# Attention block kernel, one core: the last batch's norms and the epilogue rewritten

## The chip, the cores and the metric

One core of one Trainium2 chip runs the kernel. The metric is device microseconds of one execution; before the change three runs gave 4011.88, 4012.55 and 4014.0 us (median 4012.55).

## The reference

For each of 16 images x (512 channels, 1024 pixels), all in float32:

```
qkv  = w_qkv @ x                       # 1536 x 512, then q, k, v: 8 heads of 64
sim  = (q * 64**-0.5)^T k              # per head, 1024 x 1024
out  = softmax(sim) v
y    = w_out @ out + b_out             # 512 x 1024
y    = y * rsqrt(mean_c(y*y) + 64**-0.5) * rms_scale[c]
return y + x
```

## The kernel before

One batch is one image. A batch is cut into 8 slots: a slot is a pair of heads and one half (512) of the 1024 query pixels (slot = 2 * pair + half). A slot has 16 places t = 0..15, and every engine has its own program, written out by hand, that walks the same slots and places and meets the others through semaphores. Nothing is planned at run time; what an engine does is in the order in which its function `one(body)` issues it.

In a slot TensorE (PE) makes the scores of key tile j at place t = 2j (`scores`, lines 642 and 651: 4 matmuls for 2 heads), and the products of probabilities and values at t = 1, 5, 9 and 13 (`values`, L664, two key tiles each). The last two key tiles of a slot are multiplied at t = 1 of the next slot, followed by `sums` (L583): two matmuls of ones with `prob_sum`, which give each head's softmax denominators. ScalarE (ACT) makes the exponentials (L734), two of 128x512 per key tile. GpSimd (POOL) adds the probabilities up (L1093, L1097): 14 additions of 128x512 per slot, the last ones for key tile 7. VectorE (DVE) finds row maxima of the next slot's scores, inverts the sums (L994, two reciprocals of 128x256), and makes `o_norm` (L1001). `o_norm` is split into two fp32r parts, `o_hi` by ACT (L803) and `o_lo` (L329) by POOL, in slot 6 by DVE.

The output projection of a slot is done in the slot after it, at t = 11: items O0 and O1 (L558), six fp32r matmuls each; DVE adds their result to `y_sb` (L970, 128x1024 each). So y of half 0 of a batch is complete in slot 7, y of half 1 in slot 0 of the next batch. Then come the norm's steps: four squares by ACT (L818) into `sq_a`, `sq_b`, `o_norm` and `inv_sum`; three additions by POOL (`add_squares`, L1105); a matmul of a constant 1/512 with the sum; `+ SCALE` by DVE (L981); two reciprocals (L988); a square root by ACT (`root`, L837, which loads the table of Sqrt and afterwards, L839, that of Exp); y times scale times root (L1007 on DVE, or prescaled by ACT and multiplied by POOL); residual added by POOL into `resid` (L1128), which SyncE (SP) had loaded from x (L399) and stores from there (L405). In the bodies of the 16 batches all of this lies beside the next batch's attention.

After the last batch's slot 7 nothing lies beside it: that is the epilogue, the code behind `run_bodies` in each engine's function (items R0, O0, O1, R1). In it PE does the last values, R0 (the mean of squares of half 0, one fp32 matmul on `sq_a`, L572), `sums`, O0 and O1, R1. DVE does R0's addend and reciprocals, then the sums' reciprocals from the copy that ACT made (`copy_sums`, L797), `o_norm`, four scalings of half 0, two y additions, then R1 and four scalings of half 1. POOL adds the squares of half 0, splits `o_lo`, adds the residuals of half 0, adds the squares of half 1 and adds its residuals. SP loads and stores half 0, then half 1 in the same `resid` tile.

The places before in the last batch's slot 7: `o_hi` at t = 6, `o_lo` on POOL ahead of key tile 4's additions, O0 and O1 at t = 11, squares at t = 13 and 14.

Of the kernel before, what the change touches and what calls it, by code (L numbers as in the profile page):

```python
# [13 lines left out]
P = 128  # L14
# [48 lines left out]

def items_at(slot, t, first, last):
# [22 lines left out]
    if t == 11:  # L87
        if preceding:
            out += [("O0", 0), ("O1", 2)]
# [38 lines left out]
def attention_kernel(nc, x, wqkv, wout, bias, scale, consts, out):  # L128
# [27 lines left out]
    with ctx:  # L156
# [94 lines left out]
        resid_added = sem("resid_added")  # L251
        resid_loaded = [sem(f"resid_loaded{i}") for i in range(MT)]
# [73 lines left out]
        def split_output_low(eng, done):  # L326
# [3 lines left out]
                              ).then_inc(olo_ready, 1)  # L330

# [24 lines left out]
        def _(sp):  # L356
# [100 lines left out]
        def _(pe):  # L457
# [44 lines left out]
            def item(body, slot, name, turn=None):  # L502
# [58 lines left out]
                else:  # L561
# [107 lines left out]
            def one(body):  # L669
                for slot in range(SLOTS):  # L670
# [3 lines left out]
                    for t in range(PLACES):  # L674
# [4 lines left out]
                        elif t % 4 == 1:  # L679
                            for j in (2 * g - 2, 2 * g - 1):  # L680
# [35 lines left out]
            item(last, 0, "R0")  # L716
# [7 lines left out]
        def _(act):  # L724
# [121 lines left out]
            def one(body):  # L846
                for slot in range(SLOTS):
                    for t in range(PLACES):
# [17 lines left out]
                        if t == OUTPUT_HIGH_AT[slot] and not (body.first and slot == 0):  # L866
                            split_output_high(body.b * SLOTS + slot, body)
# [3 lines left out]
                        for half in range(2):  # L871
                            if (slot, t) in SQUARE_AT[half] and (half == 0 or not body.first):
                                for m in range(MT):
                                    if (slot, t) == SQUARE_AT[half][m]:
                                        square(body, half, m)
# [22 lines left out]
            copy_sums(B * SLOTS, 0)  # L898
            root(2 * (B - 1))
# [3 lines left out]
            root(2 * (B - 1) + 1)  # L903
# [3 lines left out]
        def _(dve):  # L907
            def item(body, slot, name):
# [62 lines left out]
                elif name[0] == "R":  # L971
# [4 lines left out]
                    if name == "R1":  # L976
                        dve.wait_ge(y_scaled, scaled_before(batch, 0, 0, False) + MT)
# [41 lines left out]
            def one(body):  # L1019
                for slot in range(SLOTS):  # L1020
                    preceding = not (body.first and slot == 0)
                    for t in range(PLACES):
# [13 lines left out]
                        if t == OUTPUT_HIGH_AT[slot] and slot not in LOW_BY_GPSIMD:  # L1036
# [181 lines left out]
```

## Time and profile before

| | us |
|---|---|
| median of three runs | 4012.55 |
| the profiled execution's own time | 4015.77 |
| its span, first to last instruction | 4013.7 |
| PE busy / DVE / ACT / POOL | 3947.8 / 2890.3 / 2319.8 / 2920.6 |
| last values matmul of the last batch ends | 3969.2 |
| last probability addition on POOL ends | 3970.1 |
| last instruction on POOL (a residual addition) ends | 4011.2 |

Rows of a timeline give start, duration, engine, line, operation, output<-input, shape and count; the brackets hold how long the engine was idle before and who released it. Neighbouring instructions of one kind are merged, so that an "x4" row's duration is that of all four. PEclk is the granted TensorE clock, 1.00 for 2.4 GHz and 0.50 for 1.2 GHz.

### The profile page before, as it was taken

To read this page: it belongs to the slowest core of one execution; us is meant where nothing else is said; L and a number is where in the kernel's file an instruction comes from. 1 tells how busy PE (TensorE), PEld (TensorE's weight loads), DVE (VectorE), ACT (ScalarE), POOL (GpSimd) and SP (SyncE) were. 2 spreads that over 40 slices of the span, in tenths; PEclk is the share of its full clock that TensorE was granted. 3 is DMA by queue.
4 is the path that set the end of the run, shared out by engine and by line. 5 is a ranking of instruction groups with operands and counts; after the bars stand their busy time and mean duration, and the time that the engine had idled before them with its cause. 6 is when DMAs were issued, how large, how long until landed. Compare 5 with 4: busy or idle time off the path is not lost.

```text
span 4013.7 us, 53763 instructions
## 1 busy us (share of the span) xinstructions
PE 3947.8 (98%) x18624; PEld 2423.5 (60%) x18624; DVE 2890.3 (72%) x3279; ACT 2319.8 (58%) x4044; POOL 2920.6 (73%) x2279
## 2 busy tenths in 40 slices
PE   8999999999999999999999999999999999999996
PEld 5566665666666666666666666666566666666652
DVE  6677777777767777677777776777777777677765
ACT  4556565565655656565565655656556565565653
POOL 5678677686876768677686776867678677786866
PEclk9999999999999999999999999999999999999997
DMA  4111111111111201102011111111111111111100
GB/s 149 47 48 53 43 66 50 43 57 39 69 48 43 74 30 66 53 35 71 32 63 53 37 69 46 50 53 49 59 51 53 43 64 53 43 53 43 69 17 32
DMA packets 71275, 212.22 MB, mean 53 GB/s; under 512 B 8152, under 2 KB 8280, under 8 KB 58208
## 3 DMA queue, kind: packets, MB, share of 16 engines
q1 hardware_dynamic: 71008, 208.80, 14.8%
q8 instruction: 151, 2.47, 0.3%
q14 instruction: 116, 0.95, 0.1%
HBM read 168.92 MB, written 39.85 MB: 52 GB/s over the span
## 4 chain that ended last, share of the span: by engine, by line
PE 94%; DVE 3%; issue 2%; POOL 1%; ACT 0%; DMA 0%; SPq 0%; POOLq 0%; ACTq 0%; DVEq 0%
PE pv L664 23%; PE aux L498 17%; PE score L642 14%; PE score L651 11%; PE aux L532 9%; PE aux L558 9%; PE aux L627 6%; PE pv L583 3%; PE aux L608 2%; DVE inv_sum L994 1%; DVE maxima L936 1%; DVE k_l L929 1%; DVE y_sb L1007 0%; DVE aux L942 0%; ACT probs L734 0%
## 5 line engine op out<-in xcount | busy, mean ns | idle before, releaser
L1097 POOL TENSOR_TENSOR prob_sum<-prob_sum,probs 128x512 f32<-128x512 f32 x1536 | 1967.2, 1308 | 375.6 <-ACT probs L734 374.2
L734 ACT ACTIVATE probs<-score 128x512 f32<-128x512 f32 x2048 | 1109.1, 594 | 864.0 <-PE score L651 856.5
L942 DVE TENSOR_REDUCE aux<-aux 128x1 f32<-128x513 f32 x640 | 446.9, 698 | 836.4 <-PE aux L627 636.3
L664 PE MATMUL pv<-probs,v_sb 128*64 128x512 f32 x4096 | 993.5, 606 | 0.0
L642 PE MATMUL score<-q_hl,k_hh 128*128 128x512 f32 x2048 | 868.1, 424 | 5.8 <-ACT probs L734 5.8
L651 PE MATMUL score<-q_hm,k_l 72*128 72x512 f32 x2048 | 815.0, 398 | 0.2 <-DVE q_hm L954 0.2
L1093 POOL TENSOR_TENSOR prob_sum<-probs 128x512 f32<-128x512 f32 x256 | 338.3, 1342 | 492.4 <-ACT probs L734 492.4
L498 PE MATMUL aux<-x_hi,w_ring 128*128 128x512 f32 x2048 | 658.0, 398 | 9.7 <-DMA scale_sb<-scale 8.9
L642 PEld LDWEIGHTS score<-q_hl,k_hh 128*128 128x128 f32 x2048 | 386.9, 189 | 267.3 <-issue 154.3
L664 PEld LDWEIGHTS pv<-probs,v_sb 128*64 128x64 f32 x4096 | 248.4, 136 | 483.0 <-issue 435.3
L936 DVE TENSOR_REDUCE maxima<-aux 128x1 fp32r<-128x1024 f32 x384 | 466.3, 1214 | 0.0
L948 DVE TENSOR_REDUCE maxima<-aux 128x1 fp32r<-128x512 f32 x640 | 442.3, 691 | 22.0
L994 DVE RECIPROCAL inv_sum<-inv_sum 128x256 f32<-128x256 f32 x256 | 440.9, 1738 | 10.0 <-ACT inv_sum L797 6.5
L498 PEld LDWEIGHTS aux<-x_hi,w_ring 128*128 128x128 f32 x2048 | 386.5, 189 | 93.5 <-DMA scale_sb<-scale 8.9
L651 PEld LDWEIGHTS score<-q_hm,k_l 72*128 72x128 f32 x2048 | 388.9, 190 | 60.5 <-DVE q_hm L954 0.7
L498 PE MATMUL aux<-x_lo,w_ring 128*128 128x512 f32 x1024 | 401.1, 392 | 0.0
L532 PE MATMUL aux<-w_ring,x_hi 128*128 128x256 f32 x1984 | 361.2, 282 | 0.0
L532 PEld LDWEIGHTS aux<-w_ring,x_hi 128*128 128x128 f32 x1984 | 316.2, 191 | 11.6
L627 PEld LDWEIGHTS aux<-k_hh,q_hm 64*128 64x128 f32 x762 | 112.1, 184 | 320.2 <-issue 244.2
L627 PE MATMUL aux<-k_hh,q_hm 64*128 64x512 f32 x762 | 278.0, 444 | 10.0 <-DVE k_l L929 10.0
L532 PE MATMUL aux<-w_ring,x_lo 128*128 128x256 f32 x992 | 280.2, 283 | 0.0
L627 PE MATMUL aux<-k_hh,q_hl 64*128 64x512 f32 x762 | 277.6, 444 | 0.0
(94 smaller groups left out, 5013.1 us busy)
## 6 DMA issues: line engine op xcount, KB each, us to landing
w_ring<-w_split SPq DMA_DIRECT2D x93, 1024.0 KB, 4.8
x_stage<-x SPq DMA_DIRECT2D x128, 256.0 KB, 4.3
resid<-x SPq DMA_DIRECT2D x128, 256.0 KB, 4.2
out<-resid SPq DMA_DIRECT2D x128, 256.0 KB, 2.0
w_split<-w_ring SPq DMA_DIRECT2D x3, 1024.0 KB, 12.6
w_split<-y_sb SPq DMA_DIRECT2D x3, 1024.0 KB, 3.9
y_sb<-wqkv SPq DMA_DIRECT2D x4, 512.0 KB, 9.0
probs<-wqkv SPq DMA_DIRECT2D x2, 512.0 KB, 8.9
```

The costliest lines, as they stand in the source:

```text
L498: last = pe.matmul(out_ap, w[:, wp, k, cols], xp[:, k, xcols], start=(k == 0 and n == 0), stop=(k == KT - 1 and n == 2))
L532: last = pe.matmul(to[:, i * WCOLS:(i + 1) * WCOLS], xp[:, c, jt * P:(jt + 1) * P], w[:, wp, c, :], start=(n == 0), stop=(n == 3 * KT - 1))
L627: last = pe.matmul(bank(k + h), q_hi_at(nhalf, e, h, it), k_hh[rows, npair % 2, e, h * HALF:(h + 1) * HALF], start=True, stop=True)
L642: pe.matmul(score[e][:], k_hh[:, pair % 2, e, keys], q_hl[:, half, e, :], start=True, stop=False)
L651: pe.matmul(score[e][:], k_l1[0:D + 2 * IT, pair % 2, e, keys], q_hm[0:D + 2 * IT, half, e, :], start=False, stop=True).then_inc(score_rea ...
L664: pe.matmul(pv[half][e * D:(e + 1) * D, :], v_sb[:, pair // 2, j, (pair % 2) * P + e * D:(pair % 2) * P + (e + 1) * D], probs[:, j % 4, e, ...
L734: act.activation(probs[:, j % 4, e, :], score[e][:], ACT.Exp, scale=SOFT).then_inc(prob_ready, 1)
L936: dve.tensor_reduce(maxima[:, n:n + 1], bank(k, 2), AX_X, ALU.max).then_inc(aux_free[k], 1)
L942: dve.tensor_reduce(aux[:, first:first + 1], aux[:, k * HALF:first + 1], AX_X, ALU.max).then_inc(aux_free[k], 1)
L948: dve.tensor_reduce(maxima[:, n:n + 1], bank(k), AX_X, ALU.max).then_inc(aux_free[k], 1)
L994: dve.reciprocal(inv_sum[:, cols], inv_sum[:, cols]).then_inc(inv_ready, 1)
L1097: pool.tensor_tensor(prob_sum[:, e, :], prob_sum[:, e, :], probs[:, j % 4, e, :], ALU.add).then_inc(prob_added, 1)
```

## The change

Two constants move work within the last batch's slot 7, and the epilogue is written anew. In the last slot `o_hi` is made at t = 5, `o_lo` by DVE instead of POOL, O0 and O1 run at t = 9 ahead of the values, all four squares of half 0 at t = 9 in ACT's order, and R0 at t = 13. DVE adds the squares of half 0 (`add_squares` became a shared helper). In the epilogue ACT loads the Sqrt table once, prescales both halves of y (four operations each), and takes the last root in two column halves; DVE inverts the sums straight from PSUM, splits `o_lo`, and for half 1 does the multiplication by the root and the residual addition itself, in two column halves of 128x(4x256); the residual rows for it come into `x_stage`, a buffer of their own. R1 is four matmuls that accumulate the four squares. POOL does the multiplications and residual additions of half 0 alone.

```diff
+LAST_HIGH_AT = 5
+LAST_OUTPUT_AT = 9
@@ items_at
-    if t == 11:
+    if t == (LAST_OUTPUT_AT if last and slot == SLOTS - 1 else 11):
@@ helpers
+        def output_high_at(body, slot):
+            return LAST_HIGH_AT if body.last and slot == SLOTS - 1 else OUTPUT_HIGH_AT[slot]
+        def low_by_gpsimd(body, slot):
+            return slot in LOW_BY_GPSIMD and not (body.last and slot == SLOTS - 1)
+        def add_squares(eng, done):
+            for m in range(1, MT):
+                eng.wait_ge(sq_made, 4 * done + m + 1)
+                if m > 1:
+                    eng.wait_ge(sq_added, 3 * done + m - 1)
+                eng.tensor_tensor(sq_a[:], sq_a[:], squares[m][:], ALU.add).then_inc(sq_added, 1)
@@ sync
-            for half in range(2):
-                load_resid(B - 1, half)
-                store_half(B - 1, half)
-            wait_stored(2 * B)
+            load_resid(B - 1, 0)
+            for m in range(MT):
+                wait_piece(sp, KT + m, B - 1)
+                sp.dma_start(x_stage[:, m, :], x_v[B - 1, m, :, HALF:N]).then_inc(last_rows_loaded, 16)
+            store_half(B - 1, 0)
+            for part in range(2):
+                cols = slice(part * HALF // 2, (part + 1) * HALF // 2)
+                sp.wait_ge(last_rows_added, part + 1)
+                for m in range(MT):
+                    sp.dma_start(out_v[B - 1, m, :, HALF + part * HALF // 2:HALF + (part + 1) * HALF // 2],
+                                 x_stage[:, m, cols]).then_inc(out_stored[m], 16)
+            wait_stored(2 * B + 1)
@@ tensor, item R0 / R1
-                        pe.wait_ge(sq_added, 3 * (2 * batch + half + 1))
-                        pe.matmul(bank(k), ones_c[:].bitcast(F32), sq_a[:], start=True, stop=True
-                                  ).then_inc(aux_full[k], 1)
+                        if name == "R0":
+                            pe.wait_ge(sq_added, 3 * (2 * batch + half + 1))
+                        parts = squares[:1] if name == "R0" else squares
+                        for m, part in enumerate(parts):
+                            if name == "R1":
+                                pe.wait_ge(sq_made, 4 * (2 * batch + half) + m + 1)
+                            last = pe.matmul(bank(k), ones_c[:].bitcast(F32), part[:],
+                                             start=(m == 0), stop=(m == len(parts) - 1))
+                        last.then_inc(aux_full[k], 1)
@@ tensor, one(body), t % 4 == 1
+                            if "O0" in names:
+                                item(body, slot, "O0")
+                                item(body, slot, "O1")
                             for j in (2 * g - 2, 2 * g - 1):
...
+                            if body.last and slot == SLOTS - 1 and g == BLOCKS - 1:
+                                item(Body(epi, B - 1, False, True), 0, "R0")
@@ tensor, epilogue
-            item(last, 0, "R0")
             sums(end, 0)
@@ scalar, one(body)
-                            if (slot, t) in SQUARE_AT[half] and (half == 0 or not body.first):
...
+                                at = SQUARE_AT[half][m]
+                                if body.last and half == 0:
+                                    at = (SLOTS - 1, LAST_OUTPUT_AT)
+                                if (slot, t) == at and (half == 0 or not body.first):
+                                    square(body, half, m)
@@ scalar, epilogue
-            copy_sums(B * SLOTS, 0)
-            root(2 * (B - 1))
+            act.activation(table_back[:], ones_d[:, 0:1], ACT.Sqrt)
+            act.wait_ge(inv_ms_ready, 2 * (2 * (B - 1) + 1))
+            act.activation(rms_a[:], rms_b[:], ACT.Sqrt).then_inc(rinv_ready, 1)
+            for m in range(MT):
+                act.wait_ge(sq_made, 4 * 2 * (B - 1) + m + 1)
+                act.activation(y_sb[:, 0, m, :], y_sb[:, 0, m, :], ACT.Identity, scale=scale_sb[:, m:m + 1]
+                               ).then_inc(y_prescaled, 1)
             split_output_high(B * SLOTS)
             for m in range(MT):
                 square(end, 1, m)
-            root(2 * (B - 1) + 1)
...
+            for part in range(2):
+                cols = slice(part * HALF // 2, (part + 1) * HALF // 2)
+                act.wait_ge(inv_ms_ready, 2 * (2 * (B - 1) + 1) + part + 1)
+                act.activation(rms_a[:, cols], rms_b[:, cols], ACT.Sqrt).then_inc(rinv_ready, 1)
@@ vector, item R1
-                        dve.wait_ge(y_scaled, scaled_before(batch, 0, 0, False) + MT)
+                        dve.wait_ge(y_scaled_by_pool, scaled_before(batch, 0, 0, True) + MT)
@@ vector, epilogue
+            add_squares(dve, 2 * (B - 1))
             item(last, 0, "R0")
             for part in range(2):
                 invert(last, 0, "R0", part)
+            dve.wait_ge(sums_ready, B * SLOTS)
             for part in range(2):
-                invert_sums(end, 0, part)
+                cols = slice(part * HALF // 2, (part + 1) * HALF // 2)
+                dve.reciprocal(inv_sum[:, cols], pv[0][:, cols]).then_inc(inv_ready, 1)
             normalise(end, 0)
-            for m in range(MT):
-                scale_y(end, 0, m)
+            split_output_low(dve, B * SLOTS)
             for name in ("O0", "O1"):
                 item(end, 0, name)
             item(last, 0, "R1")
             for part in range(2):
                 invert(last, 0, "R1", part)
-            for m in range(MT):
-                scale_y(end, 1, m)
+            dve.wait_ge(y_prescaled, scaled_before(B - 1, 0, 0, True) + 2 * MT)
+            for part in range(2):
+                cols = slice(part * HALF // 2, (part + 1) * HALF // 2)
+                y = y_sb[:, 1, :, cols]
+                dve.wait_ge(rinv_ready, 2 * (B - 1) + 1 + part + 1)
+                dve.tensor_tensor(y, y, rms_a[:, cols].unsqueeze(1).to_broadcast([P, MT, HALF // 2]), ALU.mult
+                                  ).then_inc(y_scaled, 1)
+                dve.wait_ge(y_scaled, scaled_before(B - 1, 0, 0, False) + part + 1)
+                dve.wait_ge(last_rows_loaded, 16 * MT)
+                dve.tensor_tensor(x_stage[:, :, cols], x_stage[:, :, cols], y, ALU.add).then_inc(last_rows_added, 1)
@@ gpsimd, epilogue
-            add_squares(2 * (B - 1))
-            split_output_low(pool, B * SLOTS)
...
+            pool.wait_ge(rinv_ready, 2 * (B - 1) + 1)
+            scaled = scaled_before(B - 1, 0, 0, True)
+            for m in range(MT):
+                pool.wait_ge(y_prescaled, scaled + m + 1)
+                pool.tensor_tensor(y_sb[:, 0, m, :], y_sb[:, 0, m, :], rms_a[:], ALU.mult
+                                   ).then_inc(y_scaled_by_pool, 1)
+                pool.wait_ge(y_scaled_by_pool, scaled + m + 1)
+                pool.wait_ge(resid_loaded[m], 16 * (2 * (B - 1) + 1))
+                pool.tensor_tensor(resid[:, m, :], resid[:, m, :], y_sb[:, 0, m, :], ALU.add
+                                   ).then_inc(resid_added, 1)
```

## Rows read from the trace of the kernel before

**Rows 1.** The page: the chain that ended last, shares by engine.

```profile
PE 94%; DVE 3%; issue 2%; POOL 1%; ACT 0%; DMA 0%; SPq 0%; POOLq 0%; ACTq 0%; DVEq 0%
```

**Rows 2.** Windows: stretch, length, busy us (instructions) by engine, clock, DMA share, GB/s.

```profile
3855.00:3900.00 45.00, 44.77 (x198) 25.38 (x194) 31.67 (x37) 24.51 (x43) 26.48 (x22) 1.00 0.00 1
3942.00:3953.00 11.00, 9.96 (x27) 4.05 (x29) 3.90 (x5) 3.61 (x7) 3.40 (x4) 0.69 0.00 0
3953.00:3985.00 32.00, 19.69 (x70) 8.22 (x66) 12.55 (x11) 12.49 (x22) 20.88 (x17) 0.82 0.00 0
3985.00:4013.70 28.70, 6.45 (x14) 3.74 (x14) 15.66 (x13) 6.10 (x9) 17.57 (x12) 0.56 0.31 110
```

**Rows 3.** Timeline of PE, slot 7 of the last batch and the epilogue.

```profile
3945.39 3.68 PE L664 MATMUL pv<-probs,v_sb 128*64 128x512 f32 x8
...
3960.39 0.47 PE L558 MATMUL aux<-o_hi,wo_hi 128*128 128x512 f32 x1 [0.23 <-POOL o_lo L329]
...
3967.24 1.94 PE L664 MATMUL pv<-probs,v_sb 128*64 128x512 f32 x8
3974.62 2.05 PE L572 MATMUL aux<-sq_a,ones_c 128*128 128x512 f32 x2 [5.44 <-POOL sq_a L1105]
3976.59 1.98 PE L583 MATMUL pv<-prob_sum,ones_d 128*64 128x512 f32 x4
3987.33 0.77 PE L558 MATMUL aux<-o_hi,wo_hi 128*128 128x512 f32 x1 [8.76 <-POOL o_lo L329]
...
3990.41 0.40 PE L558 MATMUL aux<-o_hi,wo_lo 128*128 128x512 f32 x1
...
3997.22 2.04 PE L572 MATMUL aux<-sq_a,ones_c 128*128 128x512 f32 x2 [5.49 <-POOL sq_a L1105]
```

**Rows 4.** Timeline of DVE, the same stretch.

```profile
3954.23 0.69 DVE L1001 TENSOR_TENSOR o_norm<-inv_sum,pv 128x512 f32<-128x512 f32 x1
3962.06 2.58 DVE L970 TENSOR_TENSOR y_sb<-y_sb,aux 128x1024 f32<-128x1024 f32 x2 [7.14 <-PE aux L558]
...
3980.71 3.31 DVE L994 RECIPROCAL inv_sum<-inv_sum 128x256 f32<-128x256 f32 x2
3984.05 0.69 DVE L1001 TENSOR_TENSOR o_norm<-inv_sum,pv 128x512 f32<-128x512 f32 x1
...
3991.77 1.22 DVE L970 TENSOR_TENSOR y_sb<-y_sb,aux 128x1024 f32<-128x1024 f32 x1 [0.28 <-PE aux L558]
...
4000.03 3.37 DVE L988 RECIPROCAL rms_b<-rms_a 128x256 f32<-128x256 f32 x2
```

**Rows 5.** Timeline of ACT, the same stretch.

```profile
3979.29 1.28 ACT L837 ACT_TABLE_LOAD   x1
...
3984.77 0.63 ACT L803 ACTIVATE o_hi<-o_norm 128x512 fp32r<-128x512 f32 x1 [1.80 <-DVE o_norm L1001]
3991.52 0.63 ACT L818 ACTIVATE sq_a<-y_sb 128x512 f32<-128x512 f32 x1 [6.12 <-DVE y_sb L970]
...
4003.42 0.63 ACT L837 ACTIVATE rms_a<-rms_b 128x512 f32<-128x512 f32 x1 [7.95 <-DVE rms_b L988]
```

**Rows 6.** Timeline of POOL, the same stretch.

```profile
3960.18 9.96 POOL L1097 TENSOR_TENSOR prob_sum<-prob_sum,probs 128x512 f32<-128x512 f32 x8
...
3985.48 1.71 POOL L329 TENSOR_TENSOR o_lo<-o_norm,o_hi 128x512 fp32r<-128x512 f32 x1 [11.01 <-ACT o_hi L803]
```

**Rows 7.** Durations of DVE operations with two SBUF inputs: ns min/median/max, first and last start.

```profile
L1016 DVE TENSOR_TENSOR w_ring<-y_sb,w_ring x2: 1226/1226/1226, 6.3 to 11.5; 128x1024 fp32r<-128x1024 f32 x2
L1007 DVE SCALAR_TENSOR_TENSOR y_sb<-y_sb,scale_sb,rms_a x8: 744/1248/1759, 3984.7 to 4007.1; 128x512 f32<-128x512 f32 x8
L329 DVE TENSOR_TENSOR o_lo<-o_norm,o_hi x16: 1681/1773/1775, 234.1 to 3931.2; 128x512 fp32r<-128x512 f32 x16
```

**Rows 8.** Timeline of SP's queue: four loads, and the last store.

```profile
3993.44 1.99 SPq L399 DMA_DIRECT2D resid<-x  x4
...
4011.20 0.33 SPq L405 DMA_DIRECT2D out<-resid  x1
```

More of the change, by code:

```diff
@@ L865, in one @@
                             repeat_queries(body, slot)
-                        if t == OUTPUT_HIGH_AT[slot] and not (body.first and slot == 0):
+                        if t == output_high_at(body, slot) and not (body.first and slot == 0):
                             split_output_high(body.b * SLOTS + slot, body)
@@ L902, in _ @@
                 square(end, 1, m)
-            root(2 * (B - 1) + 1)
+            for m in range(MT):
+                act.wait_ge(sq_made, 4 * (2 * (B - 1) + 1) + m + 1)
+                act.activation(y_sb[:, 1, m, :], y_sb[:, 1, m, :], ACT.Identity, scale=scale_sb[:, m:m + 1]
+                               ).then_inc(y_prescaled, 1)
+            for part in range(2):
+                cols = slice(part * HALF // 2, (part + 1) * HALF // 2)
+                act.wait_ge(inv_ms_ready, 2 * (2 * (B - 1) + 1) + part + 1)
+                act.activation(rms_a[:, cols], rms_b[:, cols], ACT.Sqrt).then_inc(rinv_ready, 1)
         @block.vector
@@ L1035, in one @@
                                     scale_y(body, half, m)
-                        if t == OUTPUT_HIGH_AT[slot] and slot not in LOW_BY_GPSIMD:
+                        if t == output_high_at(body, slot) and not low_by_gpsimd(body, slot):
                             split_output_low(dve, body.b * SLOTS + slot)
@@ L1098, in add_probs @@
                                            ALU.add).then_inc(prob_added, 1)
-            def add_squares(done):
-                for m in range(1, MT):
-                    pool.wait_ge(sq_made, 4 * done + m + 1)
-                    if m > 1:
-                        pool.wait_ge(sq_added, 3 * done + m - 1)
-                    pool.tensor_tensor(sq_a[:], sq_a[:], squares[m][:], ALU.add).then_inc(sq_added, 1)
             def split_squares_low(done):
@@ L1120, in add_resid @@
                 done = 2 * batch + half
-                if body.plan is epi:
-                    pool.wait_ge(y_scaled, scaled_before(batch, 0, 0, False) + MT * half + m + 1)
-                elif m in SCALE_BY_GPSIMD[half]:
+                if m in SCALE_BY_GPSIMD[half]:
                     pool.wait_ge(y_scaled_by_pool, scaled_before(batch, half, m, True) + 1)
@@ L1133, in one @@
                     for j in range(STEPS):
-                        if j == OUTPUT_LOW_AT and slot in LOW_BY_GPSIMD and not (body.first and slot == 0):
+                        if j == OUTPUT_LOW_AT and low_by_gpsimd(body, slot) and not (body.first and slot == 0):
                             split_output_low(pool, body.b * SLOTS + slot)
@@ L1138, in one @@
                         elif slot in ADD_SQUARES_IN and not body.first:
-                            add_squares(2 * (body.b - 1) + slot)
+                            add_squares(pool, 2 * (body.b - 1) + slot)
                         if not body.last:
@@ L1169, in _ @@
             run_bodies(pool, one)
-            add_squares(2 * (B - 1))
-            split_output_low(pool, B * SLOTS)
-            end = Body(epi, B, False, True)
+            pool.wait_ge(rinv_ready, 2 * (B - 1) + 1)
+            scaled = scaled_before(B - 1, 0, 0, True)
             for m in range(MT):
-                add_resid(end, 0, m)
-            add_squares(2 * (B - 1) + 1)
-            for m in range(MT):
-                add_resid(end, 1, m)
+                pool.wait_ge(y_prescaled, scaled + m + 1)
[5 more added lines that the diff above has]
+                                   ).then_inc(resid_added, 1)
 def kernel(x, L0_conv_w_qkv, L0_conv_w_out, L0_conv_b_out, L0_conv_rms_scale):
```

5 lines of the change are left out of this document (2 added, 3 removed).

## The prediction

> **What bounds the kernel now.** I read the page's chain of waits first: 94% of it is PE [rows 1]. In a body window PE is busy 44.77 of 45 us (the first of [rows 2]), so bodies 0 to 14 are PE's, and the edit issues the same instructions there. I give them zero. What is left is the last batch's slot 7 and what follows. The windows say who is short there: from 3953 to 3985 PE is busy 19.69 of 32 us, from 3985 to the end 6.45 of 28.7, and no engine is busy throughout [rows 2]. This stretch is a chain of single steps, so every step on it counts in full. From the timelines I read the chain (times in the span, each start + duration):
>
> 1. POOL finishes the probability sums at 3960.18 + 9.96 = 3970.14 [rows 6].
> 2. PE could now do `sums`, but R0 stands ahead of it in PE's queue and waits for POOL's three additions of squares: 3974.62. `sums` ends at 3978.57 [rows 3].
> 3. DVE has R0's reciprocals ahead of the sums' reciprocals, which start at 3980.71; `o_norm` ends at 3984.74 [rows 4], `o_hi` at 3985.40 [rows 5], POOL's `o_lo` at 3987.19 [rows 6].
> 4. PE: O0 and O1 from 3987.33; R1 from 3997.22, behind three more POOL additions, until 3999.26 [rows 3].
> 5. DVE's reciprocals end at 4003.40 [rows 4], the root at 4004.05 [rows 5]; then four scalings and four residual additions overlap, and the last store is issued at 4011.20 [rows 8], 2.5 us before the span's end at 4013.7.
>
> **The change, part by part.**
>
> *Slot 7 (o_hi at t=5, o_lo on DVE, O0/O1 at t=9, squares behind them, R0 at t=13).* `o_norm` is there at 3954.92 [rows 4]; `o_hi` takes 0.63; `o_lo` on DVE beside a busy POOL takes 1.77 [rows 7]: 3957.35. O0 starts then instead of at 3960.39 [rows 3] and moves ahead of values 2 and 3. DVE's y additions began 1.67 us after O0's start and took 2.58 [rows 3, 4]: they end at 3961.6. Two squares are done by then, two more take 0.6 each: ACT is free at 3962.8, and it is now that key tile 5's scores are ready (values 2, 3 of 1.94 us behind O1's end at 3960.2, then 0.8 us for two score matmuls of about 0.4). So the squares cost ACT almost nothing, but key tile 6's scores wait for ACT: about 0.5 us. R0 is one fp32 matmul in two passes: 2.05 us at the low clock [rows 3], where values of 3.68 us at the low clock take 1.94 at the high one, so 1.05 here. It stands ahead of key tile 7's scores. All in all the last exponentials end at about 3969.5, and POOL's two last additions (9.96 / 8 = 1.25 each) at 3971.6, which is 1.5 later than now. Ends of the range: 3968.9 (POOL has lost an `o_lo` of about 1.3, and nothing else changes) and 3973.1 (four DVE operations each hold up POOL by some 0.5 us, and R0 waits besides). I take 3971.6. DVE's additions of squares cost 0.75 to 1.76 each (least and most of L1007 in [rows 7]); from 3961.7 they end between 3964.5 and 3967, R0 is due at 3966.6: hidden, just. R0's addend (0.69) and reciprocals (3.37) [rows 4] then lie between 3967.7 and 3971.8, beside the POOL additions.
>
> *Sums to O0.* `sums` follows the probabilities directly. PE is idle about 1 us before it, after which I expect the high clock: 1.05 us, against 1.98 at the low one [rows 3]: 3972.75. The reciprocals read PSUM directly; ACT's copy, which took 0.6, is gone. No row shows a reciprocal from PSUM. DVE's y additions with a PSUM operand take the 1.22 us that two SBUF operands take [rows 4, 7], so I take 3.31 for both, with 3.0 and 4.0 as ends. DVE starts them at 3972.8 instead of 3980.71: **7.9 us gained**. `o_norm` 0.69 and `o_hi` 0.63 are as before (ACT has long finished its root and prescalings, 3971.8 + 0.63 + 4 x 0.63 = 3975). `o_lo` is DVE's instead of POOL's: beside POOL's multiplications 1.77, alone 0.75, against 1.71 now [rows 6, 7]. I take 1.77, since POOL has eight operations of 1.25 to 1.71 to do from 3973 on, so O0 starts 7.9 earlier too: S = 3979.4.
>
> *O0 to R1.* Now: O0 at 3987.33, R1's end at 3999.26, so S + 11.9. After: the first square ends at 3992.15 [rows 5], S + 4.8, and R1's first matmul starts. Values of 1.94 us are two fp32 full-array equivalents, 0.92 each, and 1.75 each at the low clock [rows 3]. Four in a row are 3.7 or 7.2 us: S + 8.5 or S + 12.0. The three POOL additions ahead of R1 go. The clock decides: before, PE restarted at 3987.33 and ran at 0.40 us matmuls from 3990.41, 3.1 us later [rows 3]. Now the pause before R1 is under 1 us instead of 5.5, so I expect most of R1 at the high clock and allow half a microsecond: S + 9.0. **2.9 gained**; ends 3.4 and -0.1.
>
> *R1 to the end.* DVE's addend and reciprocals are as before (4.14 us from R1's end). Its wait for `y_scaled_by_pool` holds nothing up: POOL's fourth multiplication comes at about 3985, R1's addend at 3988. Now the rest is 4013.7 - 4003.40 = 10.3 us. After: the first half of the root lies beside the second reciprocal, the second beside the first multiplication. DVE does four operations of 128x1024 with two SBUF operands and POOL idle, 1.23 each [rows 7], 5.1 with gaps. The last four stores wait for the last of them together; DMA issues on SP are 0.33 [rows 8] and up to 1.99 / 4 = 0.5 apart, so the fourth is issued 1.35 us behind the first. The tail behind the last store is now 2.5; half the bytes save up to 0.3 or, as rows of 1 KB instead of 2 KB, nothing. 5.1 + 1.35 + 2.35 = 8.8. **1.5 gained**; ends 2.3 and 0. Part 0's stores go out 2.5 us earlier and are off the queue. The new x_stage loads (4 issues, 2 us of SP) and half 0's stores (its last residual addition about 3986) end long before. The Exp table load at the end is beside DVE's work in both.
>
> The Trainium skill (SBUF — State Buffer, "SBUF: two separate sides") says that a DVE operation with two SBUF inputs and a GpSimd operation that reads SBUF exclude each other for the whole instruction. The trace agrees: DVE's L1007 takes 744 ns at the least and 1759 at the most, `o_lo` on DVE beside POOL 1773 [rows 7]. It speaks against giving `o_lo` and the squares' additions to DVE; what that is worth is the third rival below.
>
> **The sum.** 7.9 + 2.9 + 1.5 = 12.3. The profiled execution's own time is 4015.77 for a span of 4013.7; I leave the 2.1 us outside the span as they are, and 4001.4 of span is 4003.5 of own time. The median of the runs is 3.2 lower than the profiled one, so the forecast is 4012.55 - 12.3 = **4000.3 us**.
>
> **Rivals.**
> - *R1 and sums at the low clock.* For it: the clock was 0.56 over the last 28.7 us, and just ahead of slot 7's second key tile it was 0.69 over 11 us although PE was busy for 9.96 of them [rows 2]. Against: the pause before R1 nearly goes. Price 3.0 (R1) + 0.9 (sums) = 3.9: 4004.2.
> - *The edit doesn't do what "one table load" says.* Squares, copies and scalings under the Sqrt table are in no row; if they need tables of their own, each change is a load of 1.28 us [rows 5]. Against it: now no load stands ahead of the squares after an Exp. Two on the chain: 4002.9.
> - *Port and queue in slot 7.* Each of the four DVE operations added there takes up to 1.77 and holds POOL, whose ten microseconds of additions set the slot's end [rows 6]; R0, if late, holds PE and key tile 7's scores. Decides when the squares' additions end behind 3966.6. Price 1.5 to 4: about 4003.
> - *Slower: the clock falls in slot 7 and stays down.* Place: PE waits for `o_lo` at t=9 and for ACT at key tile 6. If these pauses drop the clock at about 3957, as happened ahead of 3945.39 (values 3.68 instead of 1.94 [rows 3]), twelve microseconds of PE work take up to 22, and with sums and R1 low as well (3.9) the loss is 14: 4014, against before 1.5 slower. It needs the low clock through the whole slot; the clock seen there was back at 3953 [rows 2], and an episode of 7 us costs 3.5 and the kernel still faster. For it speaks little: the pauses here are 0.5 us, and O0's wait of 0.23 in the slot left the clock up [rows 3].
>
> **How the numbers follow.** What a measurement of this kernel can tell from no change is 0.2%, 8 us. Forecast 0.64; low clock in the tail 0.14; table loads 0.04; port and queue 0.09; slot at the low clock 0.03; 0.06 for disturbances of the bodies that no row shows (both signs). Best ends together (`o_lo` 1.0, R1 0.5, slot 0.7, tail 0.8): 3997.3; a range that leaves out 2 in 10 goes up to the low clock with a tail that gives nothing, 4005.5. The forecast's own range is 3998 to 4002.5. Faster by over 8 us means under 4004.5: forecast, table and most of the others, 0.85. Within: half of the low clock case, part of the port's and of the slot case: 0.11. Slower by over 8 us: 0.04.
>
> **What would show it.** O0 of slot 7 at about 3957.4; R0 done before 3968 with no wait on DVE's additions; last probability addition 3971.6; `sums` about 1 us; its reciprocals at 3972.8; O0 at 3979.4; PEclk at 1.00 in R1 and its end at 3988.4; last store issued about 3999; span 4001.4. Wrong would be it if R0 waits, if R1 takes 7 us, if the reciprocals from PSUM take over 4, or if the four halves' operations are well over 1.25 each.

## The result, and the profile after

The changed kernel takes 4000.53 us (median of 7 runs, 3997.39 to 4005.26), the kernel before 4014.0 in the same 7 rounds (4011.58 to 4014.86). The ratio is 0.997, 95% interval 0.996 to 0.9981. The gain is 13.5 us by the medians, where 12.3 were forecast. The span of the profiled execution went from 4013.7 to 3998.3.

These 15.4 us of span are not all the edit's. Some two and a half of them had come by the time slot 7 of the last batch was under way. That is drift from run to run: in the twelve traces with the same instructions up to there, the mark named here lies between 3947.85 and 3952.65. From 50 to 3930 us the granted clock was 1.00 in every window of 500 us or less, in all fourteen traces; in three of them it was 0.97 over the first 50 us, and the stretch just ahead of the mark took 12.56 to 15.31 us in the twelve (see "And the turn" below), so two parts of the drift are episodes of the clock. So I measure from one mark, the start of the values of key tiles 0 and 1 in that slot, to the end of the span, and call it the tail. The mark in the kernel before and in the changed one (PE timeline, columns as in the rows ahead of the prediction; the first block is the kernel before, the second the changed one):

```profile
3952.65 1.94 PE L664 MATMUL pv<-probs,v_sb 128*64 128x512 f32 x8
```

```profile
3950.19 1.94 PE L700 MATMUL pv<-probs,v_sb 128*64 128x512 f32 x8
...
3954.74 0.47 PE L587 MATMUL aux<-o_hi,wo_hi 128*128 128x512 f32 x1
...
3963.97 1.13 PE L607 MATMUL aux<-sq_a,ones_c 128*128 128x512 f32 x2
...
3968.97 1.08 PE L619 MATMUL pv<-prob_sum,ones_d 128*64 128x512 f32 x4 [1.08 <-POOL prob_sum L1162]
3976.51 0.76 PE L587 MATMUL aux<-o_hi,wo_hi 128*128 128x512 f32 x1 [6.46 <-DVE o_lo L336]
...
3981.50 1.07 PE L607 MATMUL aux<-sq_a,ones_c 128*128 128x512 f32 x2
...
3984.61 1.02 PE L607 MATMUL aux<-inv_sum,ones_c 128*128 128x512 f32 x2
```

The tail is 4013.7 - 3952.65 = 61.05 us before and 3998.3 - 3950.19 = 48.11 after: 12.94 less. In PE's rows the reader sees where: R0 (L607) now lies inside the slot without a wait, `sums` follows the last probability addition and takes 1.08 us instead of 1.98 [rows 3], and R1's four matmuls begin as soon as O1 ends instead of after 5.49 us. DVE's rows of the changed kernel, which answer to [rows 4]:

```profile
3953.14 1.46 DVE L336 TENSOR_TENSOR o_lo<-o_norm,o_hi 128x512 fp32r<-128x512 f32 x1 [0.70 <-ACT o_hi L843]
...
3958.92 1.12 DVE L350 TENSOR_TENSOR sq_a<-sq_a,sq_b 128x512 f32<-128x512 f32 x1
...
3960.94 0.69 DVE L350 TENSOR_TENSOR sq_a<-sq_a,inv_sum 128x512 f32<-128x512 f32 x1
...
3970.10 3.37 DVE L1127 RECIPROCAL inv_sum<-pv 128x256 f32<-128x256 f32 x2 [0.87 <-PE pv L619]
...
3974.89 1.48 DVE L336 TENSOR_TENSOR o_lo<-o_norm,o_hi 128x512 fp32r<-128x512 f32 x1 [0.70 <-ACT o_hi L843]
...
3986.39 3.37 DVE L1043 RECIPROCAL rms_b<-rms_a 128x256 f32<-128x256 f32 x2
...
3993.26 1.23 DVE L1144 TENSOR_TENSOR x_stage<-x_stage,y_sb 128x1024 f32<-128x1024 f32 x1
```

POOL, ACT and SP of the changed kernel, answering to [rows 5, 6, 8]:

```profile
3951.52 7.97 POOL L1162 TENSOR_TENSOR prob_sum<-prob_sum,probs 128x512 f32<-128x512 f32 x6
3960.98 7.94 POOL L1162 TENSOR_TENSOR prob_sum<-prob_sum,probs 128x512 f32<-128x512 f32 x6 [1.49 <-ACT probs L774]
```

```profile
3960.31 1.09 ACT L774 ACTIVATE probs<-score 128x512 f32<-128x512 f32 x2
...
3966.70 1.28 ACT L941 ACT_TABLE_LOAD   x1
```

```profile
3992.12 4.19 SPq L480 DMA_DIRECT2D out<-x_stage  x8
```

The one table load is the only one in the epilogue. The windows, answering to [rows 2], show PE and POOL busier in the same 32 us (23.63 and 24.90 us against 19.69 and 20.88), and POOL with nothing to do in the last 13 us:

```profile
3953.00:3985.00 32.00, 23.63 (x79) 12.01 (x78) 18.35 (x15) 16.12 (x29) 24.90 (x19) 0.84 0.09 33
...
3985.00:3998.30 13.30, 0.63 (x2) 0.00 (x0) 8.72 (x7) 2.39 (x5) 0.00 (x0) 0.61 0.24 79
```

### The profile page after: what moved, and what is told of

Same layout as the page of the kernel before. It is cut to its first block, busy times and chain, and to the rows that moved or that the text cites. A ratio compares the mean times of both kernels' runs of the same rounds, so it can differ in the third digit from the quotient of the medians.

```text
span 3998.3 us, 53773 instructions
## 1 busy us (share of the span) xinstructions
PE 3947.6 (99%) x18630; PEld 2424.4 (61%) x18630; DVE 2890.7 (72%) x3280; ACT 2319.5 (58%) x4048; POOL 2906.4 (73%) x2271
## 4 chain that ended last, share of the span: by engine, by line
PE 95%; DVE 3%; issue 1%; ACT 0%; DMA 0%; POOL 0%; SPq 0%; ACTq 0%; DVEq 0%; POOLq 0%
PE pv L700 23%; PE aux L527 17%; PE score L678 14%; PE score L687 11%; PE aux L561 9%; PE aux L587 9%; PE aux L663 6%; PE pv L619 3%; PE aux L644 2%; DVE inv_sum L1049 1%; DVE maxima L991 1%; DVE k_l L984 1%; DVE y_sb L1062 0%; DVE aux L997 0%; ACT probs L774 0%
## 6 DMA issues: line engine op xcount, KB each, us to landing
w_split<-w_ring SPq DMA_DIRECT2D x3, 1024.0 KB, 12.2
```

## The experiments

All are edits of the changed kernel. In the table times are in us and count from the mark; S is the start of O0 in the epilogue. Each row is one trace. From trace to trace the same code can differ by the clock: R1's end, for example, lies at S + 8.63 to S + 9.12 in the eight traces whose code from S to R1's end is the changed kernel's.

| kernel | reciprocals of sums | S | R1's end | R1's end to the end | tail |
|---|---|---|---|---|---|
| before | 28.06 | 34.68 | S + 11.93 | 14.44 | 61.05 |
| changed | 19.91 | 26.32 | S + 9.12 | 12.67 | 48.11 |
| changed, again | 19.93 | 26.34 | S + 8.98 | 12.65 | 47.97 |
| R1 on POOL's sum | 19.94 | 26.32 | S + 11.69 | 12.62 | 50.63 |
| slot 7 as before | 24.48 | 30.51 | S + 8.64 | 12.67 | 51.82 |
| and POOL adds half 0 | 28.04 | 34.07 | S + 8.63 | 12.70 | 55.40 |
| one part | 19.91 | 26.32 | S + 8.63 | 14.10 | 49.05 |
| R0 behind the slot | 21.93 | 27.97 | S + 8.63 | 12.69 | 49.29 |
| copied sums | 20.58 | 26.35 | S + 8.67 | 12.62 | 47.64 |
| copied, POOL paused | 20.60 | 26.37 | S + 9.09 | 12.63 | 48.09 |
| 24 more matmuls | 19.93 | 26.45 | S + 7.36 | 12.69 | 46.50 |
| combined | 19.92 | 25.55 | S + 7.36 | 12.33 | 45.24 |
| and the turn | 19.91 | 25.55 | S + 7.35 | 12.29 | 45.19 |
| and finer y | 19.92 | 25.55 | S + 6.42 | 12.30 | 44.27 |

**R1 on POOL's sum.**

```diff
-                        if name == "R0":
-                            pe.wait_ge(sq_added, 3 * (2 * batch + half + 1))
-                        parts = squares[:1] if name == "R0" else squares
+                        pe.wait_ge(sq_added, 3 * (2 * batch + half + 1))
+                        parts = squares[:1]
@@ gpsimd, epilogue, behind half 0
+            add_squares(pool, 2 * (B - 1) + 1)
```

> The changed kernel with R1 undone: POOL adds the squares of half 1, R1 is one matmul on sq_a. Measure: the tail, from the start of values 0 and 1 in the last slot 7 to the end of the span; it is 61.05 us before (4013.7 - 3952.65) and 48.1 after (3998.3 - 3950.19). Theory (each step of the chain counts in full): R1's end was O0's start + 9.1 in the changed kernel and + 11.9 before; the three additions come back, but the clock is still high for R1: + 10.9 to + 11.9, so tail 49.9 to 50.9. Rival (the three additions were beside something, or POOL is slow after its half 0 work): tail within 0.5 of 48.1, or over 52.

Tail 50.63, inside the theory's 49.9 to 50.9; median 4005.57 of 10 runs. One clause of the theory failed: the clock was not still high for R1. It waited for POOL and, after that pause, ran at the low clock:

```profile
3985.54 2.04 PE L604 MATMUL aux<-sq_a,ones_c 128*128 128x512 f32 x2 [5.00 <-POOL sq_a L350]
```

So squares summed by PE are worth 2.5 us, of which about one is the clock (2.04 for R1's single matmul, against 1.02 to 1.13 for each of the four).

**Slot 7 as before.**

```diff
-LAST_HIGH_AT = 5
-LAST_OUTPUT_AT = 9
+LAST_HIGH_AT = 6
+LAST_OUTPUT_AT = 11
...
+            item(last, 0, "R0")
             sums(end, 0)
```

> The changed kernel with slot 7 as before: o_hi at t=6, o_lo by POOL, O0 and O1 at t=11, squares at t=13 and 14, R0 behind the slot and ahead of sums; DVE still adds the squares and the epilogue is the new one. Theory: squares end 9.0 us behind those of the changed kernel (3969.0 against 3960.2, with 2.5 us of shift), R0 waits for DVE's third addition until about 18.5 us after the start of values 0 and 1, DVE's R0 reciprocals then stand ahead of the sums' ones, which start about 23.6 after it against 19.9 in the changed kernel: tail 51.8 (+3.7, up to +4.7 if R0 and sums run at the low clock). Rival (the whole 7.9 us came from the moves in slot 7): tail 56. Other rival (it came from DVE's additions and PSUM reads alone): tail within 1 of 48.1.

Tail 51.82, median 4005.24 of 10 runs. Both rivals are out (56, and within 1 of 48.1). That the theory's 51.8 is met to the tenth is luck: the reciprocals of the sums started at 24.48 and not at about 23.6, `sums` ran at the low clock (1.98 us), and what brought the tail back is that `o_lo` took 1.16 instead of 1.48 and that R1 ended at S + 8.64 instead of 9.12. DVE's additions beside a busy POOL took up to 2.21 us, R0 waited for them:

```profile
3961.75 2.21 DVE L350 TENSOR_TENSOR sq_a<-sq_a,sq_b 128x512 f32<-128x512 f32 x1 [1.39 <-ACT sq_b L854]
3964.24 1.40 DVE L350 TENSOR_TENSOR sq_a<-sq_a,o_norm 128x512 f32<-128x512 f32 x1 [0.28 <-ACT o_norm L854]
```

```profile
3967.46 1.36 PE L607 MATMUL aux<-sq_a,ones_c 128*128 128x512 f32 x2 [2.56 <-DVE sq_a L350]
```

**Slot 7 as before, and half 0's squares added by POOL.** The edit above, and `add_squares(pool, 2 * (B - 1))` in POOL's epilogue in place of DVE's.

> Slot 7 as before (like the second experiment) and half 0's squares added by POOL as before; sums still inverted straight from PSUM, the rest of the epilogue the changed one. Theory: POOL can add the squares only behind its last probability addition, R0 starts 22.0 us after values 0 and 1 (20.36 less 1.3 = 19.1 with DVE's additions), the sums' reciprocals at 28.1 instead of 24.5, tail 51.8 + 3.6 = 55.4. Rival (DVE's additions beside POOL, at 1.4 to 2.2 us each, are worth little): tail under 53.5.

Tail 55.40 and reciprocals at 28.04: both as expected, and the latter within 0.02 of the kernel before. One execution, 4007.44 us.

```profile
3972.25 2.04 PE L607 MATMUL aux<-sq_a,ones_c 128*128 128x512 f32 x2 [5.44 <-POOL sq_a L350]
```

PE's wait of 5.44 is the same as in [rows 3]. With this the 12.94 us are taken apart: 61.05 to 55.40 is the new epilogue (5.65), to 51.82 DVE's additions instead of POOL's (3.58), to 48.11 the moves in slot 7 (3.71). The last term is too small by the clock in R1: by S, which lies ahead of R1, the three are 0.61, 3.56 and 4.19, and the rest of the new epilogue's 5.65 lies behind S (3.30 up to R1's end, 1.74 after it). DVE's additions hold POOL up, too: POOL's last eight probability additions took 10.84 us in "slot 7 as before", with DVE's three beside them, and 9.96 here without.

**One part.** One root, one multiplication and one addition of 128x2048, four stores of 256 KB behind them, instead of two column halves.

```diff
-            for part in range(2):
+            for part in range(1):
-                cols = slice(part * HALF // 2, (part + 1) * HALF // 2)
+                cols = slice(0, HALF)
```

> The changed kernel with the last rows in one part: one root of 512 columns, one multiplication and one addition of 128x2048, four stores of 256 KB issued together at the end. Theory: the root (0.63) comes onto the chain in place of nothing, DVE's work stays at 4.8, and the last store is issued as before 1.2 to 1.5 behind the addition but moves twice the bytes, with all four behind each other on the queue (1 MB at 385 GB/s is 2.7 us, of which 1.3 us are behind the last issue): tail 48.1 + 0.6 + 1.2 = 49.9. Rival (column halves gain nothing since SP's issues set the end): tail 48.7 at most.

Tail 49.05, below the 49.9 of the theory and above the 48.7 of the rival. The tail mixes in R1, which in this execution met a better clock. From R1's end to the end it is 14.10 against 12.67: 1.43. DVE waited 0.76 for the root, and the stores end 0.78 later; DVE's own work is 0.2 shorter.

```profile
3987.70 2.29 DVE L1135 TENSOR_TENSOR y_sb<-y_sb,rms_a 128x2048 f32<-128x2048 f32 x1 [0.76 <-ACT rms_a L953]
```

**R0 behind the slot, alone.**

```diff
-                            if body.last and slot == SLOTS - 1 and g == BLOCKS - 1:
-                                item(Body(epi, B - 1, False, True), 0, "R0")
...
+            item(last, 0, "R0")
             sums(end, 0)
```

> The changed kernel with R0 alone moved behind the slot's last values (ahead of sums), everything else as changed. Theory: key tile 7's scores come 1.0 us earlier and so do the last exponentials and POOL's last addition, by 0.4 to 1.0; R0 lies in PE's pause before sums; but DVE's R0 addend and reciprocals (4.1 us) start about 1.9 us later, and the sums' reciprocals queue behind them: they start 21.6 to 22.0 us after the start of values 0 and 1 instead of 19.9, so tail 49.8 to 50.2. Rival (R0 in the slot only costs, since it holds key tile 7's scores): tail 47.1 to 47.7.

Tail 49.29 from one execution, half a microsecond below the 49.8 to 50.2 expected: the reciprocals start at 21.93 as expected, the rest is a little better (`o_lo` 1.17, R1's end at S + 8.63). But one part of my theory fell: the last additions of POOL did not come earlier. They start 10.78 us after the mark, as in the changed kernel (10.79), and run without a gap:

```profile
3960.69 7.92 POOL L1161 TENSOR_TENSOR prob_sum<-prob_sum,probs 128x512 f32<-128x512 f32 x6 [1.51 <-ACT probs L773]
```

R0 in the slot costs nothing, since from key tile 5 on POOL is behind. `sums` waits for POOL in both (0.87 here, 1.08 there).

**Copied sums.**

```diff
+            copy_sums(B * SLOTS, 0)
             act.wait_ge(inv_ms_ready, 2 * (2 * (B - 1) + 1))
@@ vector
-                dve.reciprocal(inv_sum[:, cols], pv[0][:, cols]).then_inc(inv_ready, 1)
+                invert_sums(end, 0, part)
```

> The changed kernel with the sums copied by ACT again before DVE inverts them (inv_sum <- pv, then reciprocals from SBUF). Theory: the copy stands on the chain, 0.6 us plus a hand-over, and a reciprocal costs the same from either memory (3.37 for both): tail 48.7. But R0's reciprocals end 0.9 before the sums do, so nothing else hides it. Rival (reading PSUM lengthened something else): tail 48.1 or less.

The tail was 47.64 in the one execution, where 48.7 was expected: a miss. The reciprocals began 0.67 later as expected and took 3.37 from either memory, yet S moved by 0.03 only, since `o_lo` was shorter (the rest of the 0.47 is R1, at S + 8.67 instead of 9.12). DVE, then POOL, of this kernel:

```profile
3968.84 3.37 DVE L1050 RECIPROCAL inv_sum<-inv_sum 128x256 f32<-128x256 f32 x2 [1.58 <-ACT inv_sum L837]
...
3973.62 0.83 DVE L336 TENSOR_TENSOR o_lo<-o_norm,o_hi 128x512 fp32r<-128x512 f32 x1 [0.70 <-ACT o_hi L843]
```

```profile
3972.65 1.26 POOL L1229 TENSOR_TENSOR y_sb<-y_sb,rms_a 128x512 f32<-128x512 f32 x1
```

POOL's operation ends at 3973.91 and `o_lo` at 3974.45, 0.54 later. In the changed kernel the POOL operation under way is this one, and `o_lo` ends at 3976.37, 0.56 behind its end:

```profile
3974.55 1.26 POOL L1234 TENSOR_TENSOR resid<-resid,y_sb 128x512 f32<-128x512 f32 x1
```

So `o_lo` ends by POOL's timetable and not by its own inputs', and the 0.67 us of the copy vanish in that wait. The rule of the Trainium skill that the prediction named (SBUF — State Buffer, "SBUF: two separate sides"), mutual exclusion for the whole instruction, agrees: in both traces `o_lo` was issued while POOL's operation ran and ended 0.54 and 0.56 us behind it, and alone it takes 0.69 (see "Combined").

**Copied sums, POOL paused.** The same, and POOL waits for `olo_ready` before its second residual addition.

> The changed kernel with ACT's copy of the sums back and POOL made to wait for o_lo before its second residual addition. With the copy alone the sums' reciprocals began 0.67 later, but O0 did not, since o_lo took 0.83 us instead of 1.48. Theory: o_lo waits for the POOL operation under way, and that wait hid the copy; with POOL held back o_lo takes 0.7 either way, so O0 starts 25.55 + 0.67 = 26.2 us after values 0 and 1 (25.55 with the pause and no copy). Rival (o_lo's length has nothing to do with POOL, the copy is hidden otherwise): 25.55.

S is 26.37, where 26.2 was expected, but not for the reason given: `o_lo` took 0.84, not 0.7. The pause came too late. With the copy POOL's operations stand 1.4 us later, and it was the multiplication before the paused addition (3974.22 + 1.27 = 3975.49) that held `o_lo` until 3976.04, 0.55 behind it. The clean comparison is with the combined kernel below, where the pause fits and there is no copy: S = 25.55. The copy's price is then 0.8 at most, 0.15 of it `o_lo` being held again; where `o_lo` waits for POOL anyway it is nothing. A kernel with the copy and a free `o_lo` was not run.

**24 more matmuls** between `sums` and O0, results unused.

```diff
             sums(end, 0)
+            pe.wait_ge(prob_ready, B * 128)
+            for _ in range(24):
+                pe.matmul(score[0][:], ones_c[:], x_hi[:, 0, 0:HALF], start=True, stop=True)
```

> The changed kernel with 24 more matmuls (fp32r, 128x512, into the idle bank of the scores, results unused) between sums and O0, where PE waits 6.46 us. Theory: they take 24 x 0.22 = 5.3 us of that wait, the granted clock stays at 1.00, O0 and O1 take 2.9 us instead of 5.2, and the whole chain behind them comes 2.3 us earlier (R1 is then bound by ACT's squares): tail 45.8; the spread of the runs (3997.4 to 4005.3) also gets smaller. Rival (matmuls ahead of O0 delay it, or the clock isn't on the chain since DVE's additions set the pace): tail 48.1 or longer.

Tail 46.50, 1.6 less (0.7 of the expected 2.3 missing), median 3999.89 of 5 runs from 3998.1 to 4001.0. That the spread gets smaller, as also expected, is not shown: 2.9 us here, 3.3 in 5 runs of the changed kernel (below). O0's matmuls now start at the high clock:

```profile
3972.12 5.73 PE L760 MATMUL score<-x_hi,ones_c 128*128 128x512 f32 x24
3978.75 0.47 PE L587 MATMUL aux<-o_hi,wo_hi 128*128 128x512 f32 x1 [0.90 <-DVE o_lo L336]
```

O0 and O1 take 3.0 us instead of 5.16, but R1 waits 0.69 for the first square and then is bound by its own four matmuls.

**The changed kernel again.**

> The changed kernel itself, once more, beside the next three. The tail (from the start of values 0 and 1 in the last slot 7 to the end of the span) was 48.1 us, and those of the first three experiments 50.6, 51.8 and 49.1, but their medians were 2.8 to 5.0 above the 4000.5 of the changed kernel. If the tail is all that the kernels differ in, this run's median is about 4002 and its tail 48.1, up to 1 less where R1 or O1 meets another phase of the clock. If the changed kernel's bodies are really faster than those of the experiments, it is 4000.5 again.

Median 4001.61 of 5 runs, tail 47.97. The tail repeats to 0.14 us. The medians are less exact. The runs of the experiments came in three groups, each with the kernel before beside it (medians 4013.89, 4013.58 and 4013.13). Against these the changed kernel gains 12.0 here and 13.5 in its first seven runs; the first three experiments gain 8.3, 8.7 and 10.5, 2.1, 0.6 and 1.5 less than their tails say. The 95% intervals reach some 4 to 7 us to either side, so medians do not tell single terms apart, and the tails have to.

**Combined.** The extra matmuls, the pause of POOL, and the last stores issued half by SP, half by ACT.

```diff
+                if m == 1:
+                    pool.wait_ge(olo_ready, B * SLOTS)
@@ sync, and the same on act with range(1, MT, 2)
-                for m in range(MT):
+                for m in range(0, MT, 2):
```

> The changed kernel with three edits: the 24 extra matmuls between sums and O0; POOL waits for o_lo before its second residual addition, so that DVE's o_lo (1.48 us beside POOL) runs alone; and the last eight stores are issued half by SP, half by ACT. Theory: tail 48.1 - 1.6 (matmuls, as measured) - 0.75 (o_lo takes 0.7) - 0.9 (the last of four issues is no longer 1.35 behind the first but 0.45) = 44.8. Rival (the stores are bound by their bytes, and the lock between DVE and POOL is not what lengthens o_lo): 46.5.

Tail 45.24, 0.4 above the theory's 44.8; median 3996.96 of 4 runs (3996.63 to 3998.12). `o_lo` took 0.69 us:

```profile
3975.37 0.69 DVE L336 TENSOR_TENSOR o_lo<-o_norm,o_hi 128x512 fp32r<-128x512 f32 x1 [0.70 <-ACT o_hi L846]
```

The second issuing engine gave 0.34 instead of 0.9 (last DVE instruction to the end 3.47 against 3.81). The DMA views of 11 us (40 slices of 0.275 us; busy tenths, for the combined kernel also GB/s) suggest why. With one issuing engine, in the first line (changed kernel, from 3988), there are dips between the stores; with two, below it (from 3985), the transfers stand back to back, but at 321 to 354 GB/s in full slices the bytes of a burst take most of the time that the issues took. That the bytes are the limit is read from these lines and not tested by a run:

```profile
DMA  0000000000000000009696968019697785000000
...
DMA  0000000000000000000004999991007999980000
GB/s 0 0 0 0 0 0 0 0 0 0 0 0 0 0 0 0 0 0 0 0 0 168 335 347 335 354 321 49 0 0 272 331 347 339 346 268 4 0 0 0
```

**And the turn.** At the turn from slot 6 to slot 7 of the last batch, ahead of item T (the transposed row maxima), PE waits 1.4 us for the row maxima, and after it ran at the low clock in most traces. This run is the combined kernel with five more matmuls there.

```diff
+                            if body.last and slot == SLOTS - 2 and t == PLACES - 1:
+                                pe.wait_ge(prob_ready, body.b * 128 + slot * 16 + 15)
+                                for _ in range(5):
+                                    pe.matmul(score[0][:], ones_c[:], x_hi[:, 0, 0:HALF], start=True, stop=True)
```

> The combined kernel with 5 more matmuls of the same kind ahead of item T at the end of the last batch's slot 6, where PE waits 1.4 us for the row maxima and the clock falls to 0.50 for the 6.9 us behind. Measure: from the start of values 4 and 5 in that slot 6 to the start of values 0 and 1 in slot 7; 15.2 before and in the changed kernel, 14.2 in the combined one. Theory: the clock stays at 1.00 and the eight values and four sums matmuls take half: about 12.2; median 3995. Rival (the clock falls anyway since PE waits again for the masks, or the extra matmuls delay T): 14 to 15.5 and a median of 3997 or more.

From values 4 and 5 of slot 6 to the mark it is 12.54 us (3934.07 to 3946.61; 12.2 expected), against 14.22 in the combined kernel and 15.24 in the changed one. PE's wait and the values behind it in the changed kernel, then this one:

```profile
3940.09 0.34 PE L572 MATMUL aux<-neg_ident,maxima 128*128 128x128 f32 x1 [1.40 <-DVE maxima L991]
...
3942.78 3.68 PE L700 MATMUL pv<-probs,v_sb 128*64 128x512 f32 x8
```

```profile
3938.02 1.43 PE L741 MATMUL score<-x_hi,ones_c 128*128 128x512 f32 x5 [0.22 <-ACT probs L781]
...
3940.28 0.50 PE L687 MATMUL score<-q_hm,k_l 72*128 72x512 f32 x1 [0.49 <-DVE q_hm L1022]
...
3941.32 1.94 PE L700 MATMUL pv<-probs,v_sb 128*64 128x512 f32 x8
```

Median 3994.43 of 4 runs, 18.7 below the kernel before beside it; the combined kernel was 16.6 below. One trace speaks against crediting the matmuls with all of it. "Slot 7 as before" has slot 6 unchanged and no extra matmuls, its wait is as long, and the clock stayed at 1.00 (from 3938 to 3948):

```profile
3940.96 0.30 PE L572 MATMUL aux<-neg_ident,maxima 128*128 128x128 f32 x1 [1.42 <-DVE maxima L985]
...
3943.07 1.94 PE L700 MATMUL pv<-probs,v_sb 128*64 128x512 f32 x8
```

Its turn took 12.56 us; in the other eleven traces without the five matmuls it took 13.98 to 15.31, in the two with them 12.54 and 12.53. So the pause alone does not fix what the clock does, and two traces at the high clock make it likely, but do not prove, that the matmuls hold it there. Where they do, they gain 1.4 to 2.8 us.

**And finer y.** DVE adds and ACT squares half 1 per 128 rows.

```diff
+                        if i == 0 and body.plan is epi:
+                            last.then_inc(o_part, 1)
@@ vector, items O0 and O1 of the epilogue
+                        dve.wait_ge(o_part, m // 2 + 1)
+                        dve.tensor_tensor(y_sb[:, half, m, :], y_sb[:, half, m, :], bank(k), ALU.add
+                                          ).then_inc(y_part, 1)
+                        body.full(dve, slot, name)
+                        dve.tensor_tensor(y_sb[:, half, m + 1, :], y_sb[:, half, m + 1, :], bank(k + 1), ALU.add
+                                          ).then_inc(aux_free[k], 1)
```

> The one before with y's half 1 added and squared per 128 rows: DVE adds each row block when its three matmuls are done (four additions of 128x512 instead of two of 128x1024), ACT squares it, R1 starts behind O0's second block. Theory: R1's first matmul starts at O0's start + 3.0 instead of + 3.7 and its end is at + 6.6 instead of + 7.36; median 0.7 below the one before. Rival (four additions of 0.7 cost more than two of 1.22, and each hand-over adds): + 7.4 or more.

R1's end is S + 6.42 (6.6 expected), 0.93 earlier; its matmuls follow O1's without a gap. Median 3992.94 of 4 runs (3992.57 to 3996.11), against 4013.13 of the kernel before in the same rounds: ratio 0.9953, interval 0.9938 to 0.9968. It is the best version run; the step from the one before it, 1.5 by the medians and 0.9 by the tail, is within the spread of four runs, so only the trace shows it.

## Why the prediction was right

The time came within 0.3 us of the forecast (4000.53 against 4000.3), which is closer than the working deserves. The three runs from which it started had a median of 4012.55, 1.5 below the 4014.0 of the seven beside the changed kernel, and the gain was 1.2 above the forecast 12.3; the two cancel. The tail gained 12.94. Step by step, with the terms of the sum:

- *Up to S, forecast 7.9.* The reciprocals of the sums start 8.15 earlier (28.06 to 19.91), S 8.36 earlier. The slot's inner times came close to what was worked out: O0 4.55 us after the mark (forecast 4.7), the last probability addition 18.73 after it (18.95), `sums` 1.08 (1.05), DVE's last addition of squares 2.3 us before R0 was due. Two experiments split it, by S: 34.07 to 30.51 is DVE instead of POOL for half 0's squares, 30.51 to 26.32 the moves. The other 0.6 is `o_lo` (1.16 against 1.71 in the kernel before).
- One reason in this step failed: "It stands ahead of key tile 7's scores", with the last exponentials and so POOL's last additions about 1 us later for it. R0 behind the slot left POOL where it was. What sets POOL's end is that key tile 5's scores come behind O0 and O1, which leaves POOL idle for 1.49 us, and six additions from then on, the first of them 1.79 us long and the others about 1.25. The size was right by another path.
- *`o_lo` beside POOL, 1.77 taken.* It was 1.48, by where POOL stood: it ended 0.54 to 0.56 us behind POOL's operation in the three traces read for it.
- *S to R1's end, forecast 2.9.* It was 2.81. The first square was there at S + 4.82 (forecast 4.8), but O0 and O1 ran almost wholly at the low clock (5.16 us, 4.41 before), so R1 began at S + 4.99. Its four matmuls ran at the high clock and took 4.13 with a wait of 0.21 for the third square, where 3.7 and an allowance of 0.5 stood. The allowance was for the clock in R1, and was used up by other things: there is some luck in it. In other executions of the same code R1's end lay at S + 8.63 to 9.12.
- *R1's end to the end, forecast 1.5.* It was 1.77: DVE's four operations and their gaps took 4.8, not 5.1, and from the last of them to the end it was 3.81, where 1.35 + 2.35 = 3.7 stood. By the one-part kernel the column halves are worth 1.4 of it.
- The rivals: no low clock in R1 or `sums`, no second table load, no wait of R0 on DVE, no low clock within slot 7 (1.00 from 3950 to 3968). The third rival's mechanism, that DVE and POOL hold each other up, is real, but smaller than its price of 1.5 to 4. It cost 0.8 us on the epilogue's `o_lo`. DVE's additions of squares were hardly longer for it, since two of the three met POOL's pause (0.69 each), but POOL's addition beside the last of them took 1.79 instead of about 1.27, and that half microsecond lies on the way to `sums`.

## What to carry to other kernels

Where no engine is busy throughout, take the trace as a chain, write down for each link what it waits for, and price a change link by link. Of the eight tails forecast for kernels other than the changed one, four came out within half a microsecond of the forecast or in its range (50.63, 51.82, 55.40, 45.24) and four missed by 0.5 to 1.1 (49.05, 46.50, 49.29, 47.64). A long epilogue is paid by hand-overs and by TensorE at half clock: give PE something to do in its pauses, or take the pauses away, and check which engine's queue an early result has to stand behind. Work taken off the chain pays only if the next link was not waiting for another engine anyway: the copy is the example. Compare kernels from a mark inside the trace when run-to-run drift is as large as the effect, and look at the clock behind the mark as well: it alone moved R1's end by 0.5 us here.

## What was not expected of the hardware

- After a wait of 1.40 us at the last slot 6 to slot 7 turn, PE's clock was at 0.50 for 6.9 us in the changed kernel; after one of 1.42 in "slot 7 as before" it stayed at 1.00. Why is open. With five matmuls in the wait it was at 1.00 in both traces.
- The runs' spread follows the mean granted clock, and by the traces that mean is decided in the first 50 and the last 85 us alone. In 23 runs of the kernel before, the 2 at 0.996 took 4011.1 us on average, the 15 at 0.995 4013.5, the 6 at 0.994 4015.9; of the changed kernel the one at 0.998 took 3997.4 and the one at 0.996 4005.3. With the pause ahead of O0 filled, all 5 runs stood at 0.998, where the 5 of the changed kernel again stood at 0.997.
- A reciprocal of 128x256 costs 1.69 us from PSUM as from SBUF, and a copy that was taken off the chain gave nothing, since the next operation but two waited for POOL anyway.
